# A graph layer and feed-forward kernel on one core: batch slots and gather tiles written out without loops, and one more dense group behind the last batch

## The reference

```python
xn = _layernorm(x)
# graph part: two weighted sums over the edges of each node, then attention over three branches
low  = relu(segment_sum(val_low[:, None]  * (xn @ w_low)[dst],  src, n))
high = relu(segment_sum(val_high[:, None] * (xn @ w_high)[dst], src, n))
mlp  = relu(xn @ w_mlp)
# mixer part: linear attention (k, v normalised by head), then a small MLP
out  = q @ (ln(k).T @ ln(v) / n);  mix = gelu((out + xn) @ w1 + b1) @ w2 + b2 + xn
x = x + 3 * (att0 * low + att1 * high + att2 * mlp) + mix
# feed-forward part on the half of the nodes with the largest router weight
x2n = _layernorm(x);  x = x + x2n + where(selected, (gelu(x2n @ w1f + b1f) @ w2f + b2f) * weight, 0)
```

## Time and profile before

| | |
|---|---|
| time, median of 3 runs | 2690.91 us (2688.67 to 2702.36) |
| profiled execution, its own time | 2712.93 us |
| its span, first to last instruction | 2711.2 us |
| mean granted clock of TensorE | 0.828 |
| busy: PE, PE weight load | 1922.5, 1495.5 us |
| busy: DVE, POOL, ACT | 1335.6, 1335.8, 893.7 us |
| DMA queue of POOL's indirect transfers | 14.9% of 16 engines' span |
| DMA queues of instruction blocks (q8, q14) | 28 and 25 packets |

### The profile page before, as it was taken

How to read it: one execution, slowest core, us unless ns; L and a number is a source line. 1 busy time by engine, 2 the same in 40 slices (tenths; PEclk the granted TensorE clock), 3 DMA queues, 4 the chain that set the end, 5 groups by cost and what they waited for, 6 DMA issues and landing times. The chain is left out here.

```text
span 2711.2 us, 42079 instructions
## 1 busy us (share of the span) xinstructions
PE 1922.5 (71%) x10415; PEld 1495.5 (55%) x10416; DVE 1335.6 (49%) x3575; ACT 893.7 (33%) x2606; POOL 1335.8 (49%) x1351
## 2 busy tenths in 40 slices
PE   4876877577678853467777777777777777776772
PEld 3655656576667752245654555555555555555552
DVE  8765656655556650144443344444444444443446
ACT  1653545444445550023222222222222222232223
POOL 3454455335445384655545455555455555555520
PEclk8987878778778876578888898888889887998887
DMA  2200110001011102322322232322233222223212
GB/s 73 68 24 27 32 27 12 25 26 34 18 33 33 33 5 56 90 74 71 74 69 70 69 78 74 77 76 72 68 79 76 73 72 72 77 72 79 73 31 95
DMA packets 206145, 155.15 MB, mean 57 GB/s; under 512 B 143354, under 2 KB 177676, under 8 KB 206092
## 3 DMA queue, kind: packets, MB, share of 16 engines
q0 software_dynamic: 55232, 113.59, 14.9%
q1 hardware_dynamic: 150860, 40.90, 6.8%
HBM read 139.76 MB, written 14.64 MB: 57 GB/s over the span
## 5 line engine op out<-in xcount | busy, mean ns | idle before, releaser
L1450 PE MATMUL bank<-arena 128*128 128x256 f32 (+2 forms) x5794 | 1324.8, 382 | 378.9 <-DVE arena L1082 169.9
L1450 PEld LDWEIGHTS bank<-arena 128*128 128x128 f32 x5794 | 1007.3, 211 | 667.1 <-issue 490.1
L673 POOL DMA_INDIRECT arena<-xn_rows,arena x852 | 818.1, 960 | 724.9 <-DVEq L1087 452.9
L653 POOL DMA_INDIRECT sorted_records<-arena,idx x448 | 491.9, 1098 | 518.7 <-DVE idx L816 365.6
L1082 DVE SCALAR_TENSOR_TENSOR arena<-here_nodes,arena 128x128 f32<-128x128 f32 x949 | 316.7, 352 | 564.0 <-issue 282.6
L760 DVE TENSOR_TENSOR arena<-arena 128x2940 f16<-128x2940 bf16 x28 | 47.4, 1693 | 291.6 <-ACT arena L1258 224.1
L1450 PE MATMUL bank<-arena,base 128*128 128x128 f32 (+1 forms) x568 | 110.9, 337 | 54.5 <-issue 41.2
L1450 PE MATMUL bank<-arena,side 128*128 128x128 f32 x560 | 104.9, 330 | 59.8 <-issue 58.5
L1412 ACT ACTIVATE arena<-bank 128x256 f32<-128x256 f32 x49 | 18.8, 383 | 353.8 <-PE bank L1450 160.7
L1450 PEld LDWEIGHTS bank<-arena,side 128*128 128x128 f32 x560 | 91.5, 236 | 70.8 <-issue 70.4
L1450 PEld LDWEIGHTS bank<-arena,base 128*128 128x128 f32 x568 | 93.3, 235 | 64.6 <-issue 56.1
(11 more groups left out here) (288 smaller groups left out, 2168.2 us busy)
## 6 DMA issues: line engine op xcount, KB each, us to landing
arena<-xn_rows,arena POOLq DMA_INDIRECT x852
arena<-in_x SPq DMA_DIRECT2D x24, 512.0 KB, 3.5
sorted_records<-arena,idx POOLq DMA_INDIRECT x448
xn_rows<-arena SPq DMA_DIRECT2D x12, 512.0 KB
arena<-xn_rows SPq DMA_DIRECT2D x12, 512.0 KB
out<-base SPq DMA_DIRECT2D x4, 1024.0 KB
arena<-in_L_ffn_w SPq DMA_DIRECT2D x2, 1024.0 KB, 6.4
arena<-sorted_records SPq DMA_DIRECT2D x54, 32.0 KB
```

Source lines behind the costliest of these rows:

```text
L653: pool.indirect_dma_start(rec_dram, bass.IndirectOffsetOnAxis(ap=idx[0:PR, par, u:u + 1], axis=0), stage_rec[0:PR, par, u * 8:(u + 1) * 8] ...
L673: pool.indirect_dma_start(gring[:, v % GR, :], None, xn_dram, bass.IndirectOffsetOnAxis(ap=rring[:, v, 3:4].bitcast(I32), axis=0)).then_in ...
L1450: return pe.matmul(out_, lhsT, rhs, start=start, stop=stop, **kw)
```

## The change

Four things change in the code:

- `schedule` calls `slot` 28 times without a loop for slots 0 to 27. SP's `store_xn`, `load_x` and `load_mix` and POOL's `scatter` are written out in the same way.
- SPILL goes from 2 to 3. Mixer group 10 leaves slot 24, and groups 10, 11 and 12 come in slots 28, 29 and 30, behind the last batch; slot 31 ends the last.
- In `pipeline`, the loop over stages 3 to 48 becomes a loop of four passes with TILES = 11 stages written out in each, and stages 47 and 48 written out behind it. Stage numbers in the loop are 11 * it + 3 + u.
- The loops and conditions inside `bucket_cols` stay, and so do POOL's gather loop and SP's `relay` loop.

```diff
-    SPILL = 2
+    SPILL = 3
+    TILES = 11
...
-            for n in range(2):
-                slot(n, n, n, n + 1, n - 1 if n else None, None, None)
-            with eng.Fori(1, 5) as it:
-                for par in range(2):
-                    n = 2 * it + par
-                    slot(n, par, n, n + 1, n - 1, None, None)
-            for n in range(10, MIX + 2):
-                slot(n, n % 2, n if n < NQ else None, n + 1 if n + 1 < NQ else None, n - 1 if n - 1 < NQ else None,
-                     n - MIX if n >= MIX else None, n - MIX - 1 if n > MIX else None)
-            with eng.Fori(8, 12) as it:
-                for par in range(2):
-                    n = 2 * it + par
-                    slot(n, par, None, None, None, n - MIX, n - MIX - 1)
+            for n in range(MIX):
+                slot(n, n % 2, n if n < NQ else None, n + 1 if n + 1 < NQ else None, n - 1 if 0 < n <= NQ else None, None, None)
             early = NQ - SPILL
-            for n in range(24, G):
+            for n in range(MIX, G):
                 a = n - MIX
-                slot(n, n % 2, None, None, None, a if a < early else None, a - 1 if a - 1 < early else None)
+                slot(n, n % 2, None, None, None, a if a < early else None, a - 1 if 0 < a <= early else None)
...
-            with eng.Fori(3, T) as i:
+            with eng.Fori(0, (T - 3) // TILES) as it:
+                for u in range(TILES):
+                    stage(TILES * it + 3 + u, True, True, True, True)
+            for i in range(3 + (T - 3) // TILES * TILES, T):
                 stage(i, True, True, True, True)
...
-            with sp.Fori(1, 5) as it:
-                for par in range(2):
-                    store_xn(2 * it + par)
-                    load_x(2 * it + par + 2, par)
...
+            for n in range(NQ):
                 store_xn(n)
+                if n + 2 < NQ:
+                    load_x(n + 2, n % 2)
...
-            with sp.Fori(1, 6) as it:
-                for par in range(2):
-                    load_mix(2 * it + par, par)
...
+            for n in range(NQ):
+                load_mix(n, n % 2)
...
-            with pool.Fori(0, G // 2) as it:
-                scatter(2 * it, 0)
-                scatter(2 * it + 1, 1)
+            for g in range(G):
+                scatter(g, g % 2)
```

More of the change, by code:

```diff
@@ L486, in _ @@
                 sp.dma_start(t[:, :, :], a[name].rearrange("(k p) n -> p k n", p=P)).then_inc(S("w_loaded"), 16)
-            for n in range(2):
+            for n in range(NQ):
                 store_xn(n)
-                load_x(n + 2, n)
-            with sp.Fori(1, 5) as it:
-                for par in range(2):
-                    store_xn(2 * it + par)
-                    load_x(2 * it + par + 2, par)
[L495 to L498, removed]
+                if n + 2 < NQ:
+                    load_x(n + 2, n % 2)
             sp.wait_ge(S("xn_stored"), 16 * NQ)
@@ L519, in load_mix @@
                     sp.dma_start(xs[:, :, :], quad_rows(xn_dram, a)).then_inc(S("mix_loaded"), 16)
-            load_mix(0, 0)
-            load_mix(1, 1)
-            with sp.Fori(1, 6) as it:
-                for par in range(2):
-                    load_mix(2 * it + par, par)
-            load_mix(NQ - 1, 0)
+            for n in range(NQ):
+                load_mix(n, n % 2)
             sp.wait_ge(S("mix_read"), NQ)
```

## The result

The changed kernel takes 2629.69 us (median of 4 runs, 2618.83 to 2632.0) where the kernel before takes 2696.64 us: ratio 0.9742, 95% interval 0.9695 to 0.9789. The forecast was 2646 us, 1.7% faster; it came out 2.6% faster, 67 us by the medians. The profiled execution spans 2629.1 us, 82.1 us less than before.

What follows compares the result with a forecast made beforehand. PE, ACT and DVE bound the kernel through their order, not POOL's transfers. Terms -39 - 2 - 4 = -45 us take the profiled 2712.9 to 2668 us, 2646 us for the median run; 8-in-10 range 2565 to 2765 us.

Steps and rivals of the forecast that it cites:

- Gather tiles, -39 us: Gather stages: 42 passages become straight code; half of a possible 79 us taken as gain.
- This counts in full: Gather passages: the 39 us saved on DVE all shorten the kernel, since DVE frees columns POOL waits for and feeds PE.
- lower estimate from whole stages (-25 us): Gather tiles: first-run stages 1 to 3 average 30.7 us against 31.3 for later ones, giving -25 us.
- Batch slots, -2 us: Batch part: -0.3 us for each of eight slots leaving a loop, nothing for the other eight.
- The lower end of this term, -22 us: Batch slots: the most gain allowed, if one crawl of the kind at 128.2 us goes.
- The third group, -4 us: End of batch part: group 10 moved behind the last batch saves 20.2 us ahead, costs 16 us behind.
- crawl: Stretches in batch slots and gather tiles where instructions step at about 0.7 us, cause unread; perhaps slow arrival during indirect transfers.
- the +16 end of that term: Third group: a 16 us loss if slot 24 lost only its crawl by chance, taking about 23 us anyway.
- Blocks of instructions: Written-out stages: some 120 block loads, priced at nothing while ahead of use; instruction packets rise from 53 to some 200.
- The crawl follows the transfers and not the jumps: Rival, slots and tiles: straight code leaves the crawl, only -2 - 4 remain, 2685 us; chance 0.18.
- Late new code: Rival, gather tiles: engines stand at block edges, half of 42 tiles run like stage 2, 2775 us; chance 0.25.
- The third rival: Gather tiles: straight code stops the crawl everywhere, all run like stage 1, -155 - 6, 2530 us; chance 0.13.

Runs made afterwards that it cites:

- dve_slots: Kernel before with DVE's batch slots alone written out: 2698.12 us, 0.9813 of the kernel before, on a chip with crawl.
- others_slots: Kernel before with DVE's and ACT's slots and SP's and POOL's loops written out, PE's slots looped: 2671.80 us, 0.9724 of before, with crawl.
- slots_again: Changed kernel with gather tiles still looped and SPILL = 2, on a chip with crawl: 2635.22 us, 0.9785 of the kernel before.
- after_again: The changed kernel unedited, timed again beside the kernel before on a chip with crawl: 2664.81 us, 0.9640 of it.
- tiles_straight: Changed kernel with all 49 gather stages written out, no loop over them: 2663.27 us, 0.9692 of the kernel before, with crawl.
- slots_only: Changed kernel with gather tiles still looped and SPILL = 2, on the chip without crawl: 2080.36 us, 0.9976 of the kernel before.
- spill_only: Kernel before with SPILL = 3 and all its loops kept, on the chip without crawl: 2084.47 us, 0.9996 of before.
- tiles_again: Kernel before with only the gather stage loop made four passes of eleven, on a chip with crawl: 2680.55 us, 0.9967 of before.
- pe_slots: Kernel before with PE's batch slots alone written out, on a chip with crawl: 2746.98 us, 0.9996 of before.

## Why the prediction came out as it did

**Direction and size.** Right in direction; 67 us against 45 forecast, inside the range. But that the sum came near is luck: the tiles gave 9 to 18 us instead of 39 and the slots 58 instead of 2, two errors that work against each other.

**Gather tiles, -39 us: too large.** The saving at the passages was right, its worth was not. The passages lost 1.17 us each, close to the 0.9 forecast. The step that failed is "This counts in full": 52 us were saved there, and DVE's idle time in the stages fell by 16, since waits for PE and others grew. The part alone measured 9 us, interval 19 to none; the changed kernel's profile has 18 in 44 tiles, and the profiles of the other chip 22 to 33. The lower estimate from whole stages (-25 us), which I set aside, was nearer.

**Batch slots, -2 us: this is the term that was mis-sized.** It measured 58 us. I compared looped with written-out slots of the same kernel, two pairs with opposite signs and slots that vary by 20 us each, and took the small difference as an answer. Three written-out slots beside a loop say little about a whole part written out: whether a slot is long depends on the one before. "SP's and POOL's loops give nothing" held for POOL. The written-out PE that I watched gives nothing; DVE, which I did not separate, gives 51 us. The lower end of this term, -22 us, did not reach the measurement either.

**The third group, -4 us.** Not resolved on its own: 0.9996 (0.9987 to 1.0005) without crawl, and not tried alone with it. The step that failed is that moving the group takes 20.2 us out ahead of the last batch: slot 24 was long by crawl and not by its group, as the +16 end of that term allows. With the group in it and DVE written out, it takes 26.6 us in `dve_slots`, 26.7 in `others_slots` and 35.8 in `slots_again`; without it, 40.0 in the changed kernel's first trace, 24.0 in its second (`after_again`) and 25.6 in `tiles_straight`. On the chip without crawl it takes 25.1 us with the group (`slots_only`) and 22.3 without (`spill_only`). The end behind the last batch grew by 10.1 us and not 16. By the changed kernel's first trace the move costs some 7 to 10 us.

**Blocks of instructions.** Forecast some 200 packets, measured 213, and they are hidden: `tiles_straight` and `tiles_again` show no loss beside the kernels that they are to be compared with. The Trainium skill ("Runtime: NRT & Kernel Launch", Instruction fetch mechanics) calls the crossing of a block mostly hidden, and the trace agrees; with 117 blocks in 1200 us the tiles got 1% faster. The prediction says that the trace disagrees with that section's rule on jumps, since the loop of one tile loaded nothing in 1200 us; it does not follow. In the new profile a tile's code is 0.74 MB / 39 = 19 KB on q8 and 0.59 MB / 39 = 15 KB on q14. q8 is PE's queue, as `pe_slots` raises it alone (46 packets against 28), and `dve_slots` raises q14 alone (29 against 25). The same section of the Trainium skill puts the instruction store at 128 KiB for PE and 32 KiB for most other engines. By these sizes the loop of one tile fits, and no block in 1200 us agrees with them. No term of the sum hung on it.

**Rivals.** "The crawl follows the transfers and not the jumps" holds for PE: slots in both forms crawl. Late new code did not happen: stage 2 took 29.6 us this time as new code as well, and 29.4 to 32.1 from L1146 to L1146 in all nine other traces with crawl against 35.3 in the kernel before, so its 35.6 in the earlier trace rows was crawl by chance. The third rival found no support: written-out tiles take 30.8 us and not stage 1's 27.6, and L1063 still waits 217.9 us for issue.

**What stays open.** What makes the crawl, and why one chip is without it, was not found. It runs in steps of 0.7 us, in PE and DVE, while indirect transfers are in flight. The transfers' own median time is no different without it: 0.958 us for a scatter in the kernel before and 0.959 in `spill_only`, 0.946 for a gather in both. By what path DVE's written-out slots shift the order, and which of ACT and SP adds to it, is open too, and so is what the third group does alone with crawl.

## What to carry to other kernels

Before pricing an edit against stalls that no semaphore explains, run the unchanged kernel on other chips: here that alone moved the time by 600 us, nine times what the edit gave. Where slots of equal work take turns between short and long, ask what their order in time decides and not only which engine is busiest; here writing out the slots of an engine that did not look stalled was worth 2%. To find which engine's code matters, write out one engine at a time; the stalled one was not it.

## What the runs showed of the hardware that was not expected

- The same kernel takes 2087 us on one chip and 2697 to 2755 us on three others. The granted clock of stages 4 to 46 was 1.00 on the one and 0.87 to 0.88 in the same stretch on a chip with crawl, where PE also sat idle longer between matmuls. In the crawl after 127 us PE slowed at a granted clock of 1.00, and the clock fell to 0.50 (1.2 GHz) after it.
- A kernel whose tiles load 117 instruction blocks in 1200 us runs no slower than one that loads none (`tiles_again`, 0.9967 of before).
- On the chips with crawl, writing out the slots of DVE alone takes 1.87% off the time, those of PE alone nothing (0.9996) and POOL's alone nothing (0.9988).
